# Four expert weight loads moved behind the scatter of a routed feed-forward layer, and two layer norm groups swapped between engines

## The reference

```python
h = tok(x)                                   # 64 x 14 tokens, 128 wide
h = h + attn(layernorm(h))                   # 8 heads, its own layer norm inside
h = h + ffn(layernorm(h))

def ffn(x):                                  # D_IN 128, D_HID 512, E 10 experts, top 2
    rc = gelu(conv1d_same(xt, rc_w1, rc_b1)) # 3 taps
    logits = conv1d_same(rc, rc_w2, rc_b2)   # 3 taps, one score per expert
    vals, idx = top_k(logits, 2); gates = softmax(vals)
    h = elu(x2 @ e_w1[e] + e_b1[e])          # each expert: 128 -> 512 -> 128
    y = sum over the two experts of gate * (h @ e_w2[e] + e_b2[e])
    sh = silu(conv1d_same(xt, sh_w1, sh_b1)) # shared path, 9 taps, 128 -> 512
    sh = conv1d_same(sh, sh_w2, sh_b2)       # 1 tap, 512 -> 128
    return layernorm(x + y + sh) * ln_g + ln_b
```

## Time and profile before

| | us |
|---|---|
| median of three runs | 168.0 (166.87 to 168.24) |
| the profiled execution | 167.79 |
| its span in the trace | 166.0 |
| TensorE busy | 153.9 |
| VectorE busy | 128.8 |
| GpSimd busy | 86.8 |
| ScalarE busy | 78.5 |

### The profile page before, as it was taken

The page is one execution under the profiler, slowest core; times in us unless marked ns, Lnnn a source line. Parts: engine busy times, 40 slices in busy tenths (PEclk is TensorE's granted clock), DMA queues, the critical chain, the costliest instruction groups (busy, mean ns, idle before and its releaser), DMA issues.

```text
span 166.0 us, 3076 instructions
## 1 busy us (share of the span) xinstructions
PE 153.9 (93%) x1015; PEld 136.2 (82%) x1015; DVE 128.8 (78%) x350; ACT 78.5 (47%) x194; POOL 86.8 (52%) x77
## 2 busy tenths in 40 slices
PE   7999899999999999999977799999999999999960
PEld 2898688999956568988967688989999999999930
DVE  0169999979998999789751586988989998890672
ACT  2224953220065689730304136677787787821040
POOL 1253999999999670008777200056444555550140
PEclk9999999999999999999999999999999999996995
DMA  5999999939900000000892199789999992004304
GB/s 163 320 411 390 255 231 249 190 15 190 190 2 0 0 4 2 0 0 32 229 354 88 40 277 330 272 252 285 275 335 280 321 325 110 32 32 133 108 0 111
DMA packets 19697, 28.35 MB, mean 171 GB/s; under 512 B 4982, under 2 KB 14337, under 8 KB 19682
## 3 DMA queue, kind: packets, MB, share of 16 engines
q1 hardware_dynamic: 17062, 21.47, 42.7%
q0 software_dynamic: 1696, 5.52, 13.9%
q10 hardware_dynamic: 924, 1.17, 2.7%
HBM read 19.73 MB, written 5.28 MB: 151 GB/s over the span
## 4 chain that ended last, share of the span: by engine, by line
PE 65%; POOL 18%; issue 7%; DVE 6%; ACT 2%; DVEq 0%; POOLq 0%
PE psum L716 17%; PE psum L756 14%; PE psum L744 11%; POOL prod L360 11%; PE psum L858 4%; PE psum L535 4%; PE psum L524 4%; POOL wu_l L484 2%; POOL wu_l L480 2%; POOL wu L460 2%; PE psum L558 1%; PE psum L731 1%; DVE raw L1289 1%; PE psum L852 1%; PE psum L652 1%
## 5 line engine op out<-in xcount | busy, mean ns | idle before, releaser
L509 POOL DMA_INDIRECT ys_rows<-yb,xid x22 | 21.5, 978 | 30.9 <-ACT yb L1102 18.4
L1092 ACT ACTIVATE wu<-psum,wring 128x128 f32<-128x128 f32 x92 | 26.0, 371 | 8.8 <-PE psum L744 5.7
L1411 DVE SCALAR_TENSOR_TENSOR tb<-psum,wring,wu 128x128 f32<-128x128 f32 x92 | 25.9, 344 | 0.8
L756 PE MATMUL psum<-wring,tb 128*128 128x128 f32 x184 | 25.6, 283 | 0.5 <-ACT yb L1102 0.3
L744 PE MATMUL psum<-xTb,wring 128*128 128x128 f32 x184 | 24.3, 275 | 0.0
L756 PEld LDWEIGHTS psum<-wring,tb 128*128 128x128 f32 x184 | 22.7, 194 | 1.7 <-issue 1.1
L499 POOL DMA_INDIRECT xs_rows<-xT_s,slot x14 | 14.1, 1006 | 17.7 <-DVE slot L1342 13.7
L744 PEld LDWEIGHTS psum<-xTb,wring 128*128 128x128 f32 x184 | 22.4, 192 | 0.5 <-issue 0.5
L627 PE MATMUL psum<-prod,ident_s 128*128 128x196 f32 (+1 forms) x120 | 21.6, 341 | 0.0
L627 PEld LDWEIGHTS psum<-prod,ident_s 128*128 128x128 f32 x120 | 21.1, 190 | 0.0
L360 POOL TENSOR_TENSOR prod<-es,vt 128x3136 f32<-128x3136 f32 x3 | 19.3, 6493 | 0.0
(11 more groups left out here) (183 smaller groups left out, 279.7 us busy)
## 6 DMA issues: line engine op xcount, KB each, us to landing
wring<-wexp SPq DMA_DIRECT2D x23, 514.0 KB
wu<-raw POOLq DMA_DIRECT2D x2, 1536.0 KB, 11.7
raw<-wsh SPq DMA_DIRECT2D x2, 768.0 KB, 9.3
xs_rows<-zero_s SPq DMA_DIRECT2D x1, 1472.0 KB, 15.6
ys_rows<-zero_s SPq DMA_DIRECT2D x1, 896.0 KB, 20.1
xT_s<-xT SPq DMA_DIRECT2D x2, 384.0 KB, 5.5
wu<-wsh SPq DMA_DIRECT2D x1, 768.0 KB, 7.2
xb<-xs_rows SPq DMA_DIRECT2D x1, 585.0 KB, 7.1
```

What stands on the lines that cost most here:

```text
L509: pool.indirect_dma_start(ys_dram, bass.IndirectOffsetOnAxis(ap=xid[:, j:j + 1], axis=0), yb[:, j % NY, :], None)\
L756: ins = mm(ps[Y_BANK][:, 0:D], tb[:, j % NTT, c, :], wring[:, j % NR, W2 + c * P:W2 + (c + 1) * P], start=(c == 0), stop=(c == HC - 1))
L1092: ins = A(eb[:, j % NEB, c, :], ps[U_BANKS[j % NU]][:, c * P:(c + 1) * P], ACT.Exp, bias=wring[:, j % NR, B1 + c:B1 + c + 1])
L1411: ins = V.scalar_tensor_tensor(tb[:, j % NTT, c, :], ps[U_BANKS[j % NU]][:, c * P:(c + 1) * P], wring[:, j % NR, B1 + c:B1 + c + 1], eb[:, ...
```

## The change

It has two parts. On SyncE, the loads of the first four weight blocks are no longer issued ahead of the wait for the scatter. They are issued behind it, weights 0 and 1 after the first row load, weights 2 and 3 after the second. In the layer norm ahead of the router, group 0 (three tiles) goes to ScalarE and groups 1 and 2 (two and two) to VectorE; before, ScalarE had group 1 and VectorE groups 0 and 2. The small product `nmr` now stands between the second and the third statistics.

```diff
             sp.wait_ge(S("own_done"), 1)
-            for j in range(EARLY):
-                load_weights(j)
             sp.wait_ge(S("scattered"), 16 * TOP * NT)
             for k, (a, b) in enumerate(LOADS):
                 sp.dma_start(xb[:, a:b, :], xs_dram[a * P:b * P, :].rearrange("(j p) d -> p j d", p=P)).then_inc(S(f"ld_xb{k}"), 16)
+                for j in range(k * EARLY // 2, min((k + 1) * EARLY // 2, EARLY)):
+                    load_weights(j)
             sp.wait_ge(S("m3_mm"), HC)
...
                 for n, i in enumerate(LN_GROUPS[k]):
-                    if k == 1:
+                    if k == 0:
                         pe.wait_ge(S("x3_act"), n + 1)
                     else:
-                        pe.wait_ge(S("x3_done"), (k // 2) * len(LN_GROUPS[0]) + n + 1)
+                        pe.wait_ge(S("x3_done"), (k - 1) * len(LN_GROUPS[1]) + n + 1)
...
             act.wait_ge(S("nmr_done"), 1)
-            for i in LN_GROUPS[1]:
+            for i in LN_GROUPS[0]:
                 A(x3_t[i], h2_ps[i], ACT.Identity, bias=nmr[:, 2, i:i + 1], scale=rstd[:, 2, i:i + 1]).then_inc(S("x3_act"), 1)
...
                 ln_stats(2, h2_ps, k)
-            dve.wait_ge(S("rstd_done"), ln_count(2, 1))
-            sl = tile_range(2, 1)
-            V.scalar_tensor_tensor(nmr[:, 2, sl], mv[:, 2, sl, 0], -1.0, rstd[:, 2, sl], ALU.mult, ALU.mult).then_inc(S("nmr_done"), 1)
-            for k in (0, 2):
+                if k == 1:
+                    dve.wait_ge(S("rstd_done"), ln_count(2, 0))
+                    sl = tile_range(2, 0)
+                    V.scalar_tensor_tensor(nmr[:, 2, sl], mv[:, 2, sl, 0], -1.0, rstd[:, 2, sl], ALU.mult, ALU.mult).then_inc(S("nmr_done"), 1)
+            for k in (1, 2):
                 normalise(k)
```

## The result

| | before | after |
|---|---|---|
| median of the runs | 168.0 us | 170.36 us (169.85 to 171.1) |
| ratio | | 1.0144, 95% interval 1.0102 to 1.0187 |
| profiled execution, its span | 167.79, 166.0 us | 171.02, 169.2 us |

The change costs 2.4 us, 1.4%. The forecast was 168.7 us, within 1% of the kernel before; its range held the time, its likeliest case did not.

A forecast was written before the change was run, and what follows sets the result against it. It took TensorE, busy 93% of the span, as the bound. Late weights at +0.8 us and the normalised groups at -0.1 gave +0.7 on the 168.0 us median, so 168.7 us, range 166.4 to 170.6.

The forecast's parts named there:

- likeliest case: Whole kernel: fifth weight 0.5 to 2.5 us late, clock unchanged, time 167.8 to 169.9 us; chance 0.52.
- Step 1, the scatter: GpSimd's scatter issues: taking the weights from under them gains 0 at the scatter's end, median issue 958 ns.
- Step 2, the issues: SyncE's queue behind the scatter: row load 0 issued at 94.1, row loads 2 and 3 by 100.5, weight 4 at 101.9.
- Step 3, the transfer: DMA queue: 4.16 MB at 302 GB/s puts the fifth weight's landing at 109.0 us, bounds 107.4 and 110.5.
- Step 4, who waits: TensorE's blocks: row load 1 just fits at 101.4; fifth weight 1.2 us late, 0.44 absorbed, +0.8 us left.
- (a): TensorE's new waits for late weights bring the lower clock for 3.42 us, costing 1.7: 170.4 us; chance 0.20.
- The holes: TensorE's two holes near the scatter: if weights cause them, up to 3.3 us comes earlier, costed at nothing.
- Part two: Normalised groups in the layer norm ahead of the router: -0.1 us on the first scatter, bounds -0.3 and +0.15.
- (b): Block stage loads on time: fifth weight lands before 107.8, 4.16 MB at 330 GB/s, 167.9 us; chance 0.18.
- (c): Weights beneath the scatter hold it up, so first block begins at 99.3, -1.6 us, 166.4 us; chance 0.10.

The follow-up runs named there:

- e1: Kernel before with only the layer norm groups swapped, the four weight loads left ahead of the wait for the scatter: 167.59 us, ratio 1.0021.
- e8: Changed kernel with the four weights issued under the scatter again, but behind the first sum of the shared path: 170.77 us, ratio 1.0221.
- e2: Kernel before with only the four weight loads moved, the layer norm groups left as they were: 169.58 us, ratio 1.0145.
- e3: Changed kernel with weights 0 and 1 back ahead of the wait for the scatter, weights 2 and 3 behind row load 1: 167.46 us, ratio 1.001.
- e4: Changed kernel with row load 1 issued before the four weights, all still behind the scatter: 169.77 us, ratio 1.0155.
- e6: Changed kernel with row load 1 straight behind row load 0, row load 2 behind weight 4, row load 3 behind weight 7: 168.18 us, ratio 1.0043.
- e5: Changed kernel with row load 2 behind weight 4, row load 3 behind weight 7: median 168.86 us; ratio 1.0025 over the eight runs under 170 us.

## Why the forecast was off by 1.7 us

**Step 1, the scatter: right.** Fourteen issues of 962 ns (958 in the earlier trace rows), the last at 92.16; that is 0.34 us later than before, where the third layer norm had begun 0.29 us later already.

**Step 2, the issues: right up to row load 1, then wrong.** Row load 0 went out at 94.58 (forecast 94.1), the four weights and row load 1 within 0.25 us of the forecast. But row loads 2 and 3 together took 2.40 us and weight 4 went out at 103.40, not 101.9. I take that as a sign and not a cause, since the transfers ran without a gap and a load issued earlier would have queued longer; no run holds the issue time apart from the queue, so this is argued.

**Step 3, the transfer: the rate right, the order wrong.** This is the step that failed. I divided 4.16 MB by 302 GB/s and wrote that the fifth weight "lands at about 109.0". The rate was 298 GB/s, and 4.16 MB had passed at about 109.2. The last piece of weight 4 came at 111.2, after 4.79 MB. I had treated the queue as one pipe in which a load is complete when the bytes ahead of it are through. The trace says that pieces of later loads pass the last pieces of earlier ones: 0.63 MB here, 0.69 MB at row load 1, at 300 to 350 GB/s some 2 us each. The Trainium skill ("DMA: Bandwidth & Descriptors", "Why a DMA increments its semaphore by 16 and not by 1") says that a DMA is spread over up to 16 engines and that only the full count means that all of it landed, which would make it a wait for the slowest of 16 shares. The byte counts agree with it; which share came last is not known. The upper bound of 110.5 that I gave it did not hold either (and by its own numbers, 2 us at 118 GB/s in place of 302, it should have been 110.2).

**Step 4, who waits.** Row load 1 "lands at about 101.4 ... so this just fits": it landed at 103.3 and held TensorE for 2.40 us, by the same tail. The wait for weight 0 did not show after (0.44 us with the weights alone). The fifth weight: forecast 1.2 us late and +0.8 after what is absorbed; measured 3.5 late at the fifth up projection, 0.37 absorbed by the idle time I had named (0.30 us in the earlier trace rows; my 0.44 counts from the usual distance to the next product), 3.15 left. That the fifth weight decides was right: five profiles of kernels with all rows ahead of it have the fifth up projection at 111.30, 111.29, 111.54, 110.86 and 110.14, after waits of 0.39, 1.67, 1.07, 0.27 and 1.72 us, whatever TensorE did before. With weight 4 moved up it stands at 110.12, 110.60 and 109.35 and waits for no load. So the mechanism was right and its size off by 2.3 us at the fifth up projection. That the range held the time all the same is luck: its upper end, 170.6, was made from the clock of rival (a), not from a later landing.

**The holes.** Without the four weights beneath the scatter the first hole of TensorE (2.22 us before) was gone after, and TensorE was 1.0 us ahead at the first up projection; as forecast, it was used up at once by the next wait. Over all profiles the count is this. With four weights beneath the scatter the first hole was 2.22 us (before), 0.83 (e1) and 2.94 (e8); with none or two it was absent in ten profiles and 0.64 us in e2. The second stayed in every one.

**Part two: right, on one profile of each kernel and small.** From the first statistics of the third layer norm to the low part it took 5.18 us before (53.59 to 58.77) and 5.02 after, -0.16 where -0.1 was forecast. The rows of after:

```profile
56.31 1.16 ACT L1007 ACTIVATE xT_s<-psum,nmr,rstd 128x128 f32<-128x128 f32 x3
...
57.97 0.73 DVE L1161 TENSOR_SCALAR xT_s<-psum,mv,rstd 128x128 f32<-128x128 f32 x2 [0.18 <-POOL rstd L439]
...
58.90 1.15 DVE L1281 TENSOR_TENSOR xl<-psum,xh 128x384 fp32r<-128x384 f32 x3
```

The swap alone repeats it (e1: 54.02 to 59.05, 5.03 us), and the kernel without the swap has 5.20 (e2: 53.91 to 59.11). It is too small to be seen in the times.

**The rivals.** (a) had nearly the time, 170.4, for the wrong reason: the clock did fall, but behind the wait for row load 1, which (a) did not name, and the two profiles of the changed kernel show that it didn't move the fifth up projection (111.30 with it, 111.29 without), since the landing of weight 4 covers it. (b), loads on time, is out: the loads came late in the profile, and e3, e4 and e6, which bring loads forward, change the waits or the time. Its 330 GB/s was reached from 97 to 112 us, and did not help. (c), weights holding up the scatter, is out: the scatter kept its pace with and without them (958 and 962 ns a piece), and the first row load went out no earlier. Its other half, TensorE's hole, was real but did not pay.

**What stays open.** The profiled executions differ by 3.2 us and the medians by 2.4 (1.9 on the later chip). A reading that fits, argued and not shown: where loads set the fifth block, a stretch of low clock ahead of it costs nothing, as in the second profile of the changed kernel, while the kernel before pays for it in the executions that have one. Open too are why the last pieces come so late, and what holds TensorE in its two holes.

## What to carry to other kernels

When a wait moves behind a queue of loads that is never empty, do not date a load by the bytes ahead of it: add what a profile shows as the tail, here about 0.65 MB or 2 us for a load with others close behind. So put ahead only what is needed first. Two weights fewer behind the scatter gave the whole loss back (e3); row load 1 first and 1.1 MB of late rows behind weight 4 gave two thirds of it (e6), and either alone none (e4) or about half (e5). And where a load sets a time, compare that time over several profiles: if it stays while the work ahead of it moves, no cure of that work (a higher clock, fewer holes) will show.

## What the chip showed that was not expected

- Loads that share a full queue finish late by more than their place in it: row load 1 took 3.1 us from issue to landing with only row load 0 ahead of it and four weights behind, 5.8 with two weights ahead, and 0.69 MB of later loads were through before it.
- SyncE's own issuing can slow while loads are under way: 2.40 us for two row loads, where four had taken 2.08, and 8.55 us for four weights beneath the scatter in place of 4.34. What sets it was not found.
- TensorE has a hole without a visible cause at the end of the scatter, 92 to 97 us, in every profile, weights beneath it or not (0.96, 0.38 and 0.35 us in the profile of the change). These are the rows of the changed kernel:

```profile
93.72 0.34 PE L716 MATMUL psum<-dsf_l,wu_h 128*128 128x384 f32 x1 [0.96 <-issue]
94.45 0.37 PE L716 MATMUL psum<-dsf_h,wu_l 128*128 128x448 f32 x1 [0.38 <-issue]
95.17 0.51 PE L716 MATMUL psum<-dsf_h,wu_l 128*128 128x384 f32 x2 [0.35 <-issue]
```

The matmuls come one by one about 0.7 us apart, in the middle of a product, with nothing that they wait for. In seven profiles of the experiments the lower clock followed it for some 3.4 us. What holds TensorE there was not found.
